# A decoder layer on one core: GpSimd's masks, parity columns and router constants made early in the program and kept in SBUF

## The reference

```
x = x + attention(layernorm(x))            # segments of 64, delta memory, 16 heads
x = x + cross_attention(layernorm(x), ctx) # 16 heads of 16, causal
x = x + experts(layernorm(x))              # 8 experts, the best 2 per token

cross:   q = xn @ Wq.T;  k, v = split(ctx @ Wkv.T)
         scores = where(tril, q_h @ k_h.T / sqrt(16), -max);  out = softmax(scores) @ v @ Wout.T
experts: logits = xn @ gate;  w, idx = top_k(logits, 2);  w = softmax(w)
         out = sum over the two chosen e of w_e * (silu(xn @ w0_e) * (xn @ w1_e)) @ wo_e
```

## Time and profile before

| | us |
|---|---|
| median of 3 runs (lowest, highest) | 559.17 (559.15, 560.73) |
| the profiled execution, its own time | 557.68 |
| its span, first to last instruction | 555.9 |
| PE busy | 498.3 (90%) |
| DVE busy | 342.4 (62%) |
| ACT busy | 321.3 (58%) |
| POOL busy | 144.3 (26%) |

### The profile page before, as it was taken

One profiled execution on the slowest core, in us unless ns is written; L12 is line 12 of the kernel. 1 busy time (PEld: TensorE's weight loads), 2 busy tenths in 40 slices (PEclk: granted clock), 3 DMA queues, 4 the chain that ended last, 5 costly groups with the idle time before them and its releaser, 6 DMA issues. The chain is left out here.

```text
span 555.9 us, 11854 instructions
## 1 busy us (share of the span) xinstructions
PE 498.3 (90%) x4187; PEld 416.7 (75%) x4196; DVE 342.4 (62%) x749; ACT 321.3 (58%) x762; POOL 144.3 (26%) x141
## 2 busy tenths in 40 slices
PE   8989999999999999999999699996546999999960
PEld 3778888888998888888699577774524888888850
DVE  5266666666735666666575467777473666666654
ACT  4377777778616777777661378886204444444430
POOL 5110000013100000000000438999111555555530
PEclk9999999999999999999999999999659999999995
DMA  9512112121100121110000024353213345545427
GB/s 263 164 57 60 57 57 57 57 54 46 53 2 21 58 57 57 57 57 1 0 1 2 2 79 150 115 154 115 75 47 105 121 162 170 165 143 158 157 75 226
DMA packets 24001, 48.05 MB, mean 86 GB/s; under 512 B 2960, under 2 KB 11168, under 8 KB 23968
## 3 DMA queue, kind: packets, MB, share of 16 engines
q1 hardware_dynamic: 21120, 41.17, 24.3%
q0 software_dynamic: 2240, 6.04, 3.2%
q10 hardware_dynamic: 608, 0.39, 0.3%
HBM read 42.48 MB, written 5.11 MB: 86 GB/s over the span
## 5 line engine op out<-in xcount | busy, mean ns | idle before, releaser
L659 PE MATMUL psum<-a_xt_hi,a_qk_hi 128*128 128x512 f32 x128 | 54.3, 424 | 0.0
L1403 POOL DMA_INDIRECT picks_dram<-x_wout,e_pick_row x23 | 38.7, 1683 | 52.5 <-DVE x_wout L1566 52.5
L571 DVE COPY a_weights_t<-psum 64x256 f32<-64x256 f32 x32 | 13.7, 428 | 61.5 <-PE psum L776 61.5
L659 PE MATMUL psum<-a_xt_lo,a_qk_hi 128*128 128x512 f32 x128 | 50.7, 396 | 0.0
L981 ACT ACTIVATE x_probs<-psum,x_neg_max 128x128 f32<-128x128 f32 x128 | 45.8, 407 | 8.4 <-DVE x_neg_max L1038 8.4
L659 PE MATMUL psum<-a_xt_hi,a_qk_lo 128*128 128x512 f32 x128 | 50.0, 390 | 0.0
L1444 ACT ACTIVATE e_inner_hi<-psum 128x512 fp32r<-128x512 f32 x23 | 13.8, 598 | 58.3 <-PE psum L1626 58.3
L910 POOL MEMSET x_mask<- 128x512 bf16 x1 | 0.5, 524 | 168.0 <-POOLq L248 168.0
L1617 PE MATMUL psum<-expert_w_hi,e_x_hi 128*128 x92 | 38.2, 415 | 2.2 <-DVE e_x_lo L1544 2.2
L950 POOL TENSOR_TENSOR expert_w_lo<-x_xn_t,expert_w_hi 128x1024 fp32r<-128x1024 f32 x16 | 37.7, 2358 | 1.3
L790 PE MATMUL psum<-a_weights_t,a_v 64*128 64x64 f32 x256 | 34.9, 276 | 3.4 <-issue 2.5
(11 more groups left out here) (236 smaller groups left out, 1500.2 us busy)
## 6 DMA issues: line engine op xcount, KB each, us to landing
x_k_t<-in_expert_wo SPq DMA_DIRECT2D x23, 512.0 KB
a_qk_raw<-in_wqk SPq DMA_DIRECT2D x32, 256.0 KB, 2.7
x_xn_t<-in_expert_w SPq DMA_DIRECT2D x16, 512.0 KB, 3.9
a_wv_raw<-in_wv SPq DMA_DIRECT2D x17, 256.0 KB, 2.8
x_sb<-in_x SPq DMA_DIRECT2D x2, 512.0 KB, 4.9
x_k_t<-in_wo SPq DMA_DIRECT2D x1, 1024.0 KB, 10.3
x_v<-in_wo SPq DMA_DIRECT2D x1, 1024.0 KB, 12.8
xn_dram<-xn SPq DMA_DIRECT2D x1, 1024.0 KB, 4.4
```

Of the source, the lines that this page charges most:

```text
L571: dve.tensor_copy(weights_t[SEG:P, :, 0:2, :], t_ps[SEG:P, :, 0:2, :]).then_inc(wt_ready, 1)
L659: last = pe.matmul(out, pick_l(left[a], k), pick_r(right[b], k), start=start and n == 0, stop=n == 3 * KD - 1, skip_group_check=not start)
L1403: pool.indirect_dma_start(out=picks_dram, out_offset=bass.IndirectOffsetOnAxis(ap=pick_row[:, tile:tile + 1], axis=0), in_=y_rows[:, slot, ...
```

## The change

The tiles `x_mask`, `x_parity`, `e_iota_i`, `e_iota`, `e_tile_start`, `e_spare_row`, `e_ones` and `e_before` belong to the whole program instead of to one block. GpSimd makes them all in the attention block, after its four weight splits and ahead of its first quarter of the output weight. The float iota, `tile_start` and `spare_row`, which VectorE made, are made by GpSimd too. The waits for them stay where they were, with new counts. `e_reached`, a tile of the router, now lies in the memory of `x_v`.

```
+        self.x_mask = self.sb("x_mask", [P, 4, S], BF16)
+        self.parity = self.sb("x_parity", [P, 2], F32)
+        self.iota_i = self.sb("e_iota_i", [P, P + 1], I32)
...
+            def cross_constants(pool):
+                consts = c.x_consts
+                pool.memset(c.x_mask[:, :, :], 0.0).then_inc(consts, 1)
+                pool.memset(c.parity[:, :], 0.0).then_inc(consts, 1)
+                pool.wait_ge(consts, 2)
+                pool.affine_select(out=c.x_mask[:, :, :], in_=c.x_mask[:, :, :], compare_op=ALU.is_ge, fill=MASKED, base=0,
+                                   pattern=[[0, 4], [-1, S]], channel_multiplier=1).then_inc(consts, 1)
...
+                                pool.wait_ge(consts, n)
+                                pool.affine_select(out=col, in_=col, compare_op=ALU.is_gt, fill=fill, base=base,
+                                                   pattern=[[0, 1]], channel_multiplier=-1).then_inc(consts, 1)
...
+            def router_constants(pool):
+                consts = c.e_consts
+                pool.memset(c.ones[:, :], 1.0).then_inc(consts, 1)
+                pool.memset(c.before[:, :], 1.0).then_inc(consts, 1)
+                pool.iota(c.iota_i[:, 0:P], pattern=[[1, P]], base=0, channel_multiplier=0).then_inc(consts, 1)
...
+                pool.tensor_copy(c.iota[:, :], c.iota_i[:, :]).then_inc(consts, 1)
...
             split_qk(1, 1)
             split_wv(1, 1)
+            cross_constants(pool)
+            router_constants(pool)
...
         def _(pool):
-            pool.memset(mask[:, :, :], 0.0).then_inc(consts, 1)
             pool.memset(v_pad[:, :, :, :], 0.0).then_inc(v_zeroed, 1)
-            pool.memset(parity[:, :], 0.0).then_inc(consts, 1)
             pool.wait_ge(v_zeroed, 1)
-            pool.wait_ge(consts, 2)
...
-            pool.wait_ge(consts, n)
...
-            dve.wait_ge(iota_made, 2)
+            dve.wait_ge(consts, 8)
             dve.memset(ones_f[:, :], 1.0)
             dve.memset(either[:, B, :], 0.0)
-            chained(dve.tensor_copy(iota[:, :], iota_i[:, :]))
-            chained(dve.tensor_scalar(tile_start[:, :], iota[:, 0:TILES + 1], float(P), None, ALU.mult))
-            dve.tensor_scalar(spare_row[:, :], tile_start[:, 0:TILES], iota[:, P:P + 1], float(PICKS * P), ALU.add, ALU.add)
```

More of the change, by code:

```diff
@@ L56, in __init__ @@
         self.logits = self.sb("e_logits", [P, B, NE], F32)
+        self.x_mask = self.sb("x_mask", [P, 4, S], BF16)
+        self.parity = self.sb("x_parity", [P, 2], F32)
+        self.iota_i = self.sb("e_iota_i", [P, P + 1], I32)
+        self.iota = self.sb("e_iota", [P, P + 1], F32)
+        self.tile_start = self.sb("e_tile_start", [P, TILES + 1], F32)
+        self.spare_row = self.sb("e_spare_row", [P, TILES], F32)
+        self.ones = self.sb("e_ones", [P, P], BF16)
+        self.before = self.sb("e_before", [P, P], BF16)
+        self.x_consts, self.e_consts = self.sem("x_consts"), self.sem("e_consts")
     def sb(self, name, shape, dt, ctx=None):
@@ L316, in split_wv @@
                                    ALU.subtract).then_inc(wv_lo_ready, 1)
+            def cross_constants(pool):
[5 more added lines that the diff above has]
+                                   pattern=[[0, 4], [-1, S]], channel_multiplier=1).then_inc(consts, 1)
+                n = 3
+                for odd in range(2):
+                    col = c.parity[:, odd:odd + 1]
+                    for start in range(HD * odd, P, 2 * HD):
+                        for base, fill in ((start, CROSS_SCALE), (start + HD, 0.0)):
+                            if base < P:
+                                pool.wait_ge(consts, n)
+                                pool.affine_select(out=col, in_=col, compare_op=ALU.is_gt, fill=fill, base=base,
+                                                   pattern=[[0, 1]], channel_multiplier=-1).then_inc(consts, 1)
+                                n += 1
+                c.n_x_consts = n
@@ new lines, in router_constants @@
+            def router_constants(pool):
[3 more added lines that the diff above has]
+                pool.iota(c.iota_i[:, 0:P], pattern=[[1, P]], base=0, channel_multiplier=0).then_inc(consts, 1)
+                pool.wait_ge(consts, 3)
+                pool.iota(c.iota_i[:, P:P + 1], pattern=[[0, 1]], base=0, channel_multiplier=1).then_inc(consts, 1)
+                pool.affine_select(out=c.before[:, :], in_=c.before[:, :], compare_op=ALU.is_gt, fill=0.0, base=0,
+                                   pattern=[[1, P]], channel_multiplier=-1).then_inc(consts, 1)
+                pool.wait_ge(consts, 5)
+                pool.tensor_copy(c.iota[:, :], c.iota_i[:, :]).then_inc(consts, 1)
+                pool.wait_ge(consts, 6)
+                pool.tensor_scalar(c.tile_start[:, :], c.iota[:, 0:TILES + 1], float(P), None, ALU.mult).then_inc(consts, 1)
+                pool.wait_ge(consts, 7)
+                pool.tensor_scalar(c.spare_row[:, :], c.tile_start[:, 0:TILES], c.iota[:, P:P + 1], float(PICKS * P),
+                                   ALU.add, ALU.add).then_inc(consts, 1)
@@ L834, in sb @@
         return c.sb(name, shape, dt, phase)
-    wq, wout, k_t, v_sb = c.wq, c.wout, c.k_t, c.v
+    wq, wout, k_t, v_sb, mask, parity, consts = c.wq, c.wout, c.k_t, c.v, c.x_mask, c.parity, c.x_consts
     xn_t = sb("x_xn_t", [P, KD, B * S], F32)
@@ L1262, in expert_phase @@
     xn, logits = c.xn, c.logits
[L1263 to L1268, removed]
+    iota, tile_start, spare_row, ones, before, consts = c.iota, c.tile_start, c.spare_row, c.ones, c.before, c.e_consts
     ones_f = sb("e_ones_f", [P, NE], F32)
@@ L1379, in _ @@
         def _(pool):
[L1380 to L1388, removed]
             pool.wait_ge(xn_stored, 16)
@@ L1583, in _ @@
         def _(pe):
[L1584 removed]
+            pe.wait_ge(consts, 8)
             pe.wait_ge(either_ready, 1)
```

20 lines of the change are left out of this document (2 added, 18 removed).

## The result

| | before | after |
|---|---|---|
| median of runs taken together, us | 559.01 (20 runs) | 556.49 (20 runs) |
| ratio to before, 95% interval | 1 | 0.9928 (0.9900 to 0.9956) |
| the profiled execution, its own time | 557.68 | 556.47 |
| its span | 555.9 | 554.7 |
| mean granted clock | 0.964 | 0.951 |

The changed kernel is faster by 0.72%, 4.0 us of 559 (2.5 to 5.6). Single executions scatter by several us around either median and the ratio leaves the disturbed ones out, so it is the better figure; 0.9928 of 559.17 is 555.1. Forecast were 553.5, and 551.6 to 556.4 as the range. 555.1 lies in the range, 1.6 above the forecast; the plain median of 556.49 lies 0.1 above the range's end.

What follows compares the result with a forecast made beforehand. TensorE, busy 90%, was taken to lose time standing still at two block borders behind GpSimd's constants. 2.48 + 1.47 + 1.75 = 5.70 off 557.68 gives 551.98; with the 1.49 offset 553.5 us, range 551.6 to 556.4.

Steps and rivals of the forecast that it cites:

- Sign and chances: Whole kernel: faster (below 557.5 us) 0.90, same 0.06, slower (above 560.8 us) 0.04.
- rival A: The low clock returns elsewhere, so only the two borders' waits, 4.23 us, are gained: 554.9 us; chance 0.24.
- Term one: Start of cross attention: TensorE's standstill for GpSimd's parity columns ahead of the mask matmul goes, 2.48 us gained.
- Clock term: Cross attention, third projection: without the parity standstill the low clock stretch disappears, 1.47 us gained.
- Term two: Router start: VectorE's wait for GpSimd's iota and three operations leave the path to the maxima, 1.75 us gained.
- Constants early: Attention block: GpSimd makes the constants in free time (the cover), 16.60 to 30.18, ending at 25.3: cost 0.
- Collision: End of cross attention: VectorE's layernorms against GpSimd's subtraction; both chains move by 3.95 us, so 0 counted.
- Rival B: End of cross attention: GpSimd's last piece comes earlier, layernorms take under 3 us, total 552.0 us; chance 0.12.
- Rivals C and D: First: waits replaced at both borders, 557.6, chance 0.06; second: new SBUF addresses slow the attention loop, 562.5 at 3%, chance 0.04.
- The offset: Whole kernel: the median of the runs lies 1.49 us above the profiled execution; this was left in the forecast.

Runs made afterwards that it cites:

- warm kernels: The kernel before and the changed kernel, each with filler matmuls in TensorE's gaps at the borders (the former also in the parity gap): 1.0037 and 0.9912 of before.
- router_only: The kernel before with only the router's constants made early, mask and parity left in cross attention: 1.0010 of before.
- before_gapfill: The kernel before with 5 filler matmuls of 256 columns in the parity gap ahead of the first mask matmul: 1.0010 of before.
- layout_only: The kernel before with the eight tiles and e_reached at their new addresses, every instruction where it was: 0.9986 of before.
- before_warm: The kernel before with filler matmuls in the barrier gap, the parity gap, late cross attention, before the logits and in the router: 1.0037 of before.
- after_again: The changed kernel run and profiled once more, nothing altered: 0.9939 of before, median 555.77 us.
- last_low: The changed kernel with GpSimd's last subtraction for the expert weights replaced by a memset: one run of 551.17 us, no ratio.
- cover_gone: The changed kernel with the parity columns made four times over, so GpSimd is late for the output weight: four runs, 551.23 to 565.97 us, no ratio.
- cross_only: The kernel before with only the mask and parity columns made early, the router's constants left in place: 0.9946 of before.
- three_ops: The changed kernel with the three operations on the iota back on VectorE: 0.9923 of before.
- after_tuned: The changed kernel with all TensorE gaps filled by idle matmuls, resized and moved according to an earlier profile: 0.9889 of before, median 552.35 us.
- border_fill: The changed kernel with 2 filler matmuls of 512 columns in the barrier gap alone: 0.9906 of before, median 553.01 us.

## Why the prediction was right or wrong

- **Sign and chances.** Faster by 4.0 us, in the 0.90 for faster. Of the cases, what was measured is rival A: it said 4.23. That the figure comes so close is partly luck: A let the clock neither give nor take, but in the profiles it did both, as below.
- **Term one, 2.48.** Right: 2.44 from 8.16 to 5.72 where neither profile has a bare low stretch before the mask, 2.38 between the warm kernels up to the layernorms. From the block's start to the first exponential it is 2.43 between the warm kernels (10.93 and 8.50), so the followers (selections, table load, first exponential) had the slack that was read.
- **Clock term, 1.47.** Wrong, and this is the step that failed: "With no standstill before 318, I take the low stretch to be gone." It did not go; it moved in front of the projections, behind the barrier gap that the change leaves. In 5 of 6 profiles it stands there and costs 1.44 up to the first exponential (9.93 or 9.94 in all five against 8.50). In the same five the low level came back at 380.3 to 381.5, ahead of the layernorms, and took another 0.9 to 1.2; the sum had no term for that. So their layernorms come after 76.0 to 76.3, no sooner than router_only's 76.00, which still had its parity wait. The row that could have warned was in the text: the 2.4 us at the barrier was named as a lower bound of 0 and then given too little weight. What the trace of before could not show is that the stretch had two places: of the four profiles with parity made behind the barrier and the barrier gap open, router_only and before_gapfill have it behind the barrier, before and layout_only behind the parity gap. The first place was free because of the parity wait (76.00 in router_only, 76.14 in before_warm with no low stretch at all), the second cost 1.6 to 1.8 (77.8 to the layernorms). The Trainium skill, in TensorE: Matmul & The Clock Gate, section What you observe, has the moment of one such change, from slow to fast in a row of matmuls, vary by 500 ns from run to run. Here more varies: the low stretch was there in one profile of the changed kernel and missing in the other, 1.44 us at this border.
- **What a bare stretch is worth** was sized well. From the first exponential to the layernorms it is 66.68 before and 65.21 to 65.26 in the seven profiles without a low stretch in between, which makes 1.47 behind the parity gap (layout_only: 1.6), and 1.44 behind the barrier. What failed is whether it disappears.
- **Term two, 1.75.** 1.81 measured, twice: 2.39 to 0.58 and 2.40 to 0.59. It is a wait of 1.18 and operations of 0.63; the forecast's lower bound of 0.61 was the operations alone. router_only's time doesn't confirm it. The time of after fits it, since 2.4 and 1.8 make 4.2, but only if the clock took about as much after as before.
- **Constants early, 0.** Right, and with a little more room than claimed: they ended at 24.93 (estimated 25.3), and with the cover taken away nothing moved. The parity selects took 4.76 there against 4.42 behind the barrier. The sigma that GpSimd might hold up started at 21.40 instead of 21.23, and by 68 us the heads were 0.04 behind the profile of before. One rival is open. The low level near 33 us, which cost after_again 2.8, is in 5 of the 10 profiles with constants made early and in none of the 4 without. That can be chance; no run tests it.
- **Collision, 0.** Within its bound: 3.41 and 4.30 in the two profiles after, 4.20 before. That the subtraction causes it was argued; last_low shows it. Undisturbed the four take 1.38, not the 1.64 of the prediction. The Trainium skill, in SBUF — State Buffer, section Who interferes with whom, lets GpSimd and a VectorE instruction in a two-port mode hold each other off for the whole instruction. The layernorms of 1.38 without the subtraction agree; that they ran in such a mode no run here shows. Rival B did not come in these two profiles; in cover_gone the same layernorms took 2.84, under B's mark of 3.
- **Rivals C and D.** No follower was late, and the first maximum stood 0.10 behind the other engines' start; the layout alone is 0.9986 (0.9953 to 1.0020).
- **The offset.** The profile of before had the low level only from 392.7; layout_only, router_only, cross_only, three_ops and both profiles of the changed kernel had it from some moment between 380.3 and 384.9 on. From the layernorms to the logits, before took 12.05 and layout_only 13.15. So one lucky profile was the sum's base, and beside it the tail of after looks up to 1.1 us worse.

Open: why the low level falls behind the barrier gap in most profiles and not in after_again; why it comes back before the layernorms in just those profiles of the changed cross attention that had it at the barrier; why router_only's time doesn't show its 1.8 us; and whether filling the parity gap alone could have paid with fewer rows.

## What to carry to other kernels

A wait on the path can hide a slow clock ahead of it. When the wait goes, don't book the slow stretch as gone while another standstill before it remains: price it at both places, and look at two profiles before believing either. A gap on TensorE that can't be closed may be worth filling with idle matmuls: after_tuned's 0.9889 is the lowest ratio here, but not clear of the plain change. They must be sized from the timeline so that the next engine doesn't wait for them.

## What the runs showed of the hardware

- GpSimd's dependent 128x1 selects take 0.32 to 0.33 us each (4.76 for 15, 20.00 for 60) in the attention block, and 0.29 at the start of cross attention (4.42 for 15).
- The same three operations cost 0.29, 0.31 and 0.42 on GpSimd and 0.23, 0.18 and 0.24 on VectorE; early and off the path, the slower engine costs nothing that the runs show.
- Standing idle for 2.42 us ahead of the same instructions was followed within 1.3 us by the low level in 5 of the 6 profiles of the changed border and not in the sixth. Filled down to 0.71, it was followed by full clock in every profile (four, before_warm with them; one of the four, border_fill, would perhaps have had it anyway).
- Four layernorms of 128x256 on VectorE took 2.84 to 4.30 us beside GpSimd's subtraction of 128x1024 (2.3 to 2.5 us), and 1.38 with a memset of 0.95 in its place.
